# Moving half of GpSimd's adds into an accumulating DMA, and one field from VectorE to ScalarE, in a DLRM tower with a CIN

## The reference

```python
e = stack([tbl_f[ids[:, f]] for f in range(39)], axis=1)     # 512 x 39 x 16
prev = x = e
for k in range(3):                                           # 128 units each
    z = einsum('bmd,bhd->bdmh', x, prev).reshape(b, D, m * h)
    t = transpose(einsum('bdc,co->bdo', z, ws[k]) + bs[k], (0, 2, 1))
    t = t / sqrt(sum(t * t, axis=(-2, -1), keepdims=True))
    logit.append(t); prev = t
z = sum(concatenate(logit, axis=1), axis=-1)
h = relu(concatenate([z, dense_ctx], axis=1) @ W_top1 + b_top1)
y = relu(h @ W_top2 + b_top2) @ W_top3
```

## Time and profile before

| | |
|---|---|
| median of 3 runs | 1061.88 us (1060.4 to 1062.07) |
| profiled execution | 1062.48 us, its span 1060.8 us |
| PE busy | 1028.2 us (97%) |
| PEld busy | 782.4 us (74%) |
| DVE busy | 983.6 us (93%) |
| ACT busy | 791.3 us (75%) |
| POOL busy | 865.9 us (82%) |
| DMA | 46.10 MB, 43 GB/s on average |

### The profile page before, as it was taken

How to read it: one execution, slowest core, us unless ns; L and a number is a source line. 1 busy time by engine, 2 the same in 40 slices (tenths; PEclk the granted TensorE clock), 3 DMA queues, 4 the chain that set the end, 5 groups by cost and what they waited for, 6 DMA issues and landing times.

```text
span 1060.8 us, 17970 instructions
## 1 busy us (share of the span) xinstructions
PE 1028.2 (97%) x4320; PEld 782.4 (74%) x4320; DVE 983.6 (93%) x3344; ACT 791.3 (75%) x2655; POOL 865.9 (82%) x729
## 2 busy tenths in 40 slices
PE   2999999999999999999999999999999999999998
PEld 0477777878777787877778787777878777788884
DVE  2589999999999999999999999999999999999993
ACT  3476877868788786868778687777868778788872
POOL 6777988889898888988888898888889888577770
PEclk9999999999999999999999999999999999999999
DMA  5650030302303030120303012030301203000000
GB/s 188 129 143 12 3 88 3 89 2 52 96 4 88 3 87 4 21 71 2 89 3 87 5 28 64 3 89 2 85 7 17 74 3 89 1 1 1 2 1 1
DMA packets 75892, 46.10 MB, mean 43 GB/s; under 512 B 55689, under 2 KB 58633, under 8 KB 75658
## 3 DMA queue, kind: packets, MB, share of 16 engines
q1 hardware_dynamic: 68487, 38.59, 15.2%
q10 hardware_dynamic: 2179, 5.07, 1.4%
q0 software_dynamic: 5120, 1.29, 1.4%
HBM read 42.99 MB, written 1.94 MB: 42 GB/s over the span
## 4 chain that ended last, share of the span: by engine, by line
PE 48%; POOL 19%; DVE 18%; issue 9%; ACT 5%; DMA 1%; POOLq 0%; DVEq 0%; SPq 0%; ACTq 0%
POOL sums L432 14%; DVE sums L946 12%; PE acc L778 8%; PE bank_d L722 7%; PE bank_d L723 6%; PE bank_d L724 6%; PE bank_a L724 6%; PE bank_a L722 6%; PE bank_a L723 6%; POOL gathered L415 5%; ACT scaled L560 4%; DVE bank_d L946 2%; DVE sums L965 1%; ACT sums L560 1%; PE turned L799 1%
## 5 line engine op out<-in xcount | busy, mean ns | idle before, releaser
L432 POOL TENSOR_TENSOR sums<-sums,scaled 128x512 f32<-128x512 f32 (+1 forms) x512 | 645.1, 1262 | 133.4 <-ACT scaled L560 97.4
L946 DVE SCALAR_TENSOR_TENSOR sums<-bank_d,x_col,sums 128x128 f32<-128x128 f32 x2304 | 654.2, 339 | 29.3 <-PE bank_d L724 20.2
L560 ACT ACTIVATE scaled<-bank_a,x_col 128x128 f32<-128x128 f32 x1920 | 551.5, 385 | 139.8 <-PE bank_a L724 132.7
L722 PE MATMUL bank_d<-w_hi,prev_lo 128*128 128x512 f32 x640 | 288.0, 450 | 6.2 <-DVE sums L965 4.7
L722 PE MATMUL bank_a<-w_hi,prev_lo 128*128 128x512 f32 (+1 forms) x640 | 263.9, 412 | 2.6 <-issue 1.3
L724 PE MATMUL bank_d<-w_hi,prev_hi 128*128 128x512 f32 x640 | 252.5, 394 | 0.0
L723 PE MATMUL bank_d<-w_lo,prev_hi 128*128 128x512 f32 x640 | 252.1, 394 | 0.0
L724 PE MATMUL bank_a<-w_hi,prev_hi 128*128 128x512 f32 (+1 forms) x640 | 245.3, 383 | 0.0
L723 PE MATMUL bank_a<-w_lo,prev_hi 128*128 128x512 f32 (+1 forms) x640 | 245.1, 383 | 0.0
L560 ACT ACTIVATE sums<-bank_a,x_col 128x128 f32<-128x128 f32 x512 | 146.1, 369 | 76.8 <-PE bank_a L724 75.9
L415 POOL DMA_INDIRECT gathered<-in_table,idx x160 | 177.2, 1108 | 28.5 <-issue 18.3
(11 more groups left out here) (84 smaller groups left out, 528.2 us busy)
## 6 DMA issues: line engine op xcount, KB each, us to landing
x_pairs<-x_scratch SPq DMA_DIRECT2D x135, 156.0 KB
x_pairs<-x_scratch SPq DMA_DIRECT2D x96, 78.0 KB
gathered<-in_table,idx POOLq DMA_INDIRECT x160
x_sq<-x_scratch SPq DMA_DIRECT2D x32, 64.0 KB
x_pairs<-x_scratch SPq DMA_DIRECT2D x92, 22.0 KB
x_scratch<-gathered SPq DMA_DIRECT2D x16, 72.0 KB
w_raw<-in_w ACTq DMA_DIRECT2D x1, 1024.0 KB, 5.1
w_raw<-in_w ACTq DMA_DIRECT2D x1, 896.0 KB
```

What stands on the lines that cost most here:

```text
L432: nc.gpsimd.tensor_tensor(out=sums[:, n % SUMS, 0:w, :], in0=sums[:, n % SUMS, 0:w, :], in1=scaled[:, a - 1, 0:w, :], op=ALU.add).then_inc ...
L560: op = nc.scalar.activation(to[:, i, :], bank_a[at % A_RING][:, i * UNITS:(i + 1) * UNITS], ACT.Copy, scale=x_of(c, q, a * PER_BANK + i))
L722: nc.tensor.matmul(to, lo, w_h, start=True, stop=False)
L946: nc.vector.scalar_tensor_tensor(out=taken(n, u) if u in LEFT else total, in0=taken(n, u), scalar=x_of(c, q, A_FIELDS + u), in1=total, op0 ...
```

## The change

In jobs 11 to 116 ("far" jobs) GpSimd no longer adds four slots. It issues one DMA on its own queue that adds slots 3 and 4 onto slots 1 and 2 in SBUF (`accum_op=ALU.add`, 128 partitions of 4096 bytes, 512 KB), and four and five banks later it adds slots 1 and 2 onto `sums`. So that there is time for it, the A banks run ahead by 12 banks instead of 7; the lead grows by one bank a job in jobs 6 to 10 and shrinks again after job 116. Odd far jobs have slots of their own (`scaled_odd`), in the room of the raw weights. GpSimd's gathers move from A places 1 and 2 to 3 and 4 of a job from job 11 on. In all jobs the fields are split 20 to ScalarE and 19 to VectorE, so the bank of three fields is now VectorE's last. The places of `high`, `low`, `make_pairs` and the norms stay.

```diff
-A_FIELDS = A_BANKS * PER_BANK - 1
+A_FIELDS = A_BANKS * PER_BANK
-LEAD = 7
+LEAD, FAR_LEAD = 7, 12
+FAR_FROM, FAR_TO = 11, NJ - 12
+LEADS = [min(max(LEAD, LEAD + n - 5), FAR_LEAD, max(LEAD, FAR_LEAD + FAR_TO - n)) for n in range(NJ + 1)]
+FAR_ADDS = {1: A_BANKS - 1, 2: A_BANKS}
+def a_first(n):
+    return A_BANKS * n + LEADS[n]
+def a_count(n):
+    return a_first(n + 1) - a_first(n) if n + 1 < NJ else A_BANKS
+for _n in range(NJ):
+    for _a in range(1, A_BANKS):
+        if not is_far(_n):
+            ADDS_BEHIND[A_BANKS * _n + _a].append((_n, _a))
+        elif _a in FAR_ADDS:
+            ADDS_BEHIND[A_BANKS * _n + A_BANKS - 1 + FAR_ADDS[_a]].append((_n, _a))
...
+            def add_banks(at):
+                if at >= A_BANKS * NJ:
+                    return
                 n, a = divmod(at, A_BANKS)
-                pool.wait_ge(a_scaled, at + 1)
-                if a > 1:
-                    pool.wait_ge(a_added, ADDS * n + a - 1)
-                w = a_fields_of(a)
-                nc.gpsimd.tensor_tensor(out=sums[:, n % SUMS, 0:w, :], in0=sums[:, n % SUMS, 0:w, :],
-                                        in1=scaled[:, a - 1, 0:w, :], op=ALU.add).then_inc(a_added, 1)
+                if is_far(n) and a == A_BANKS - 1:
+                    pool.wait_ge(a_scaled, at + 1)
+                    nc.gpsimd.dma_start(pair_of(n, 1), pair_of(n, 3), accum_op=ALU.add).then_inc(pair_added[n % 2], 16)
+                for n, a in ADDS_BEHIND[at]:
+                    if is_far(n):
+                        pool.wait_ge(pair_added[n % 2], pairs_added_by(n))
+                    else:
+                        pool.wait_ge(a_scaled, at + 1)
+                    if a > 1:
+                        pool.wait_ge(a_added, ADDED[n, a - 1])
+                    w = PER_BANK if is_far(n) else a_fields_of(a)
+                    nc.gpsimd.tensor_tensor(out=sums[:, n % SUMS, 0:w, :], in0=sums[:, n % SUMS, 0:w, :],
+                                            in1=scaled_of(n, a)[:, 0:w, :], op=ALU.add).then_inc(a_added, 1)
...
-                for a in range(A_BANKS):
-                    add_bank(A_BANKS * n + LEAD + a)
-                    if 1 <= a <= per_step and first + a - 1 < GATHERS:
-                        gather(it + 2, first + a - 1)
+                begin = 1 if n < FAR_FROM else 3
+                for a in range(max(a_count(n), A_BANKS)):
+                    if a < a_count(n):
+                        add_banks(a_first(n) + a)
+                    if begin <= a < begin + per_step and first + a - begin < GATHERS:
+                        gather(it + 2, first + a - begin)
...
-                    if n >= 1:
-                        act.wait_ge(a_added, ADDS * (n - 1) + a)
-                    to = scaled[:, a - 1, :, :]
+                    was = n - 1 if n < FAR_FROM else n - 2
+                    if n == FAR_FROM:
+                        act.wait_ge(w_lo_made[1], len(W_PIECES[1]))
+                        act.wait_ge(w_lo_made[2], len(W_PIECES[2]))
+                    elif is_far(was) and a > max(FAR_ADDS):
+                        act.wait_ge(pair_added[was % 2], pairs_added_by(was))
+                    elif was >= 0:
+                        act.wait_ge(a_added, ADDED[was, a] if (was, a) in ADDED else added_all(was))
+                    to = scaled_of(n, a)
...
-                        bank_for_act(A_BANKS * n + LEAD + a)
-                        a += 1
+                        until = a + 1 if place < len(PATTERN) - 1 else a_count(n)
+                        while a < until:
+                            bank_for_act(a_first(n) + a)
+                            a += 1
...
-                    dve.wait_ge(a_added, ADDS * (n + 1))
+                    dve.wait_ge(a_added, added_all(n))
```

More of the change, by code:

```diff
@@ L46 @@
 D_BANKS = BANKS - A_BANKS
-A_FIELDS = A_BANKS * PER_BANK - 1
+A_FIELDS = A_BANKS * PER_BANK
 D_FIELDS = FIELDS - A_FIELDS
-ADDS = A_BANKS - 1
 LEFT = (D_FIELDS - 3, D_FIELDS - 2)
@@ L200, in cin_kernel @@
         identity = sb("identity", [128, 128])
-        w_raw = {k: sb(f"w{k}_raw", [128, FIELDS, UNITS]) for k in (1, 2)}
+        used = 28
+        with ExitStack() as first_life:
+            w_raw = {k: first_life.enter_context(nc.sbuf_tensor(f"w{k}_raw", [128, FIELDS, UNITS], f32)) for k in (1, 2)}
+        scaled_odd = []
+        for k in (1, 2):
+            sb(f"raw_rows{k}", [128, used, UNITS])
+            scaled_odd.append(sb(f"scaled_odd{k}", [128, 2, PER_BANK, UNITS]))
+            sb(f"raw_rest{k}", [128, FIELDS - used - 2 * PER_BANK, UNITS])
         w_hi = {k: sb(f"w{k}_hi", [128, FIELDS, UNITS], f32r) for k in (1, 2)}
@@ L285, in cin_kernel @@
         a_added = sem("a_added")
+        pair_added = [sem(f"pair_added{parity}") for parity in range(2)]
         d_ready = sem("d_ready")
@@ L323, in cin_kernel, with scaled_of, pair_of, pairs_added_by @@
         TOP_LOADS = 2 * 3 + 2
+        def scaled_of(n, a):
+            if n < FAR_FROM or n % 2 == 0:
+                return scaled[:, a - 1, :, :]
+            return scaled_odd[(a - 1) // 2][:, (a - 1) % 2, :, :]
+        def pair_of(n, a):
+            first = scaled[:, a - 1:a + 1, :, :] if n % 2 == 0 else scaled_odd[(a - 1) // 2][:, :, :, :]
+            return first.rearrange("p a i u -> p (a i u)")[:, 0:(PER_BANK + a_fields_of(A_BANKS - 1)) * UNITS]
+        def pairs_added_by(n):
+            return 16 * ((n - FAR_FROM) // 2 + 1)
         def a_fields_of(a):
@@ L464, in _ @@
                 gather(2, j)
-            for at in range(LEAD):
-                add_bank(at)
+            for at in range(LEADS[0]):
+                add_banks(at)
             for n in range(NJ):
@@ L668, in _ @@
                                  ACT.Copy).then_inc(prev_hi_made[1], 1)
-            for at in range(LEAD):
+            for at in range(LEADS[0]):
                 scale_bank(at)
-                if at == LEAD - 2:
+                if at == LEADS[0] - 2:
                     square_x(1)
             for n in range(NJ):
-                for a in range(A_BANKS):
-                    scale_bank(A_BANKS * n + LEAD + a)
+                for a in range(max(a_count(n), A_BANKS)):
+                    if a < a_count(n):
+                        scale_bank(a_first(n) + a)
                     if (n, a) in W2_HIGH_AT:
```

14 lines of the change are left out of this document (10 added, 4 removed).

## The result

The changed kernel takes 1078.41 us in the median of 4 runs (1075.81 to 1079.59); the kernel before, run beside it, 1061.97 (1060.4 to 1062.07). The ratio is 1.0155 [1.0134, 1.0176]: 1.5% slower. Forecast were 1052.4 us, in a range that ends at 1070. In the profiled executions 16.05 us were added (1062.48 to 1078.53). In the changed kernel the lines have moved: L722 to L724 are now L804 to L806, L946 is L1031, L965 L1050, L914 L999, L432 L503, L437 L508, L560 L641 and L765 L847; L494 is the issue of the accumulating DMA.

A forecast was written before the change was run, and what follows sets the result against it. TensorE was taken as within 2% of its own work, stopped by VectorE. From 1062.48 us, -14.3 (VectorE), -2 and -1 (ends), +7.8 (longer lead) gave 1053.0, as a median 1052.4; 8-in-10 range 1042 to 1070.

The forecast's parts named there:

- The accumulating DMA: GpSimd's new transfer: taken at 4.5 us, some 7 us in the load burst, cost 0, bounds 0 and 39 us.
- VectorE's part: VectorE loses one field a job and `make_pairs` gets shorter; its stops of TensorE vanish, -1.1 us a round, -14.3 us.
- What the longer lead costs: Position 5, first A bank of layer 1: TensorE waits 0.6 us for `prev_lo` in each of 13 rounds, +7.8 us.
- ScalarE's part: ScalarE gains a field a job, 2.1 us a round, 78% busy to 82%; costed at nothing, hidden under idle time.
- GpSimd's part: GpSimd's adds fall from 5.04 to 2.61 us a job plus one DMA issue; load no bound, its order can be.
- Ends: Stretch ahead of job 11, -2 us (0 to -4), and the last job's D banks, -1 us.
- The bound of 5.5 us: GpSimd's loop of issue, transfer and add must fit in 7.78 us; a transfer over 5.5 us makes GpSimd the bound.
- The mild burst form: Rival: only transfers in the load burst are late enough to reach TensorE, some 1.5 us a round, 1072 us; chance 0.08.
- The slow transfer throughout: Rival: a transfer of 6.2 us makes GpSimd's loop the bound in 106 jobs, 1127 us; chance 0.15.
- the floor: Rival: `prev_lo` is in time because ScalarE's queue runs earlier, 1044.6 us; chance 0.17.
- the eaten gain: Rival: `low` is late by another 0.7 us and the new wait eats the gain, 1061.5 us; chance 0.10.
- the last rival: VectorE isn't what stops TensorE, so the change only adds its own wait: within 2 us of 1062; chance within another rival's 0.10.

The follow-up runs named there:

- e3: Changed kernel without the accumulating DMA: slots 3 and 4 of far jobs left out of the sum, lead 12, the split and two adds kept; 1053.95 us, ratio 0.9926.
- e5: Changed kernel with the load burst made small (64-byte rows instead of 2048 from the third chunk on) and the head's weights loaded in round 14; 1056.93 us, ratio 0.9962.
- e7: Changed kernel with the head's weights loaded in round 14 instead of round 3; 1074.37 us, ratio 1.0136.
- e6: Changed kernel with far jobs at positions 0 and 1 added by GpSimd alone, four adds, all other far jobs by the DMA; 1060.81 us, ratio 0.9993.
- e1: Kernel before with only the field split changed, 20 to ScalarE and 19 to VectorE; 1069.0 us, ratio 1.0067.
- e2: Changed kernel with its lead of 12 banks, but GpSimd adds all four slots itself and there is no accumulating DMA; 1107.6 us, ratio 1.0436.
- e4: Changed kernel with `high` and `low` of layer 1 moved from position 5, place 0, to position 4, place 3; 1087.02 us, ratio 1.0237.
- e10: Changed kernel with a lead of 11 banks instead of 12 and the two adds three and four banks behind instead of four and five; 1111.7 us, ratio 1.049.
- e9: Changed kernel with far jobs at positions 0 and 1 added by GpSimd alone and the head's weights loaded in round 14; 1058.24 us, ratio 0.9973.

## Why the prediction was wrong

**The step that failed** is in "The accumulating DMA": "a transfer doubled there to some 7 us is late by 1.5 us in those, and the slack of three D banks takes it up. I cost it at 0". The length was well guessed (median 5.97 us for the burst's first job, 6.57 in the chain of a round, up to 8.2), the upper bound of 39 us held. The cost of 0 didn't. e3 and e5 take the collision away in two ways, one without the transfer and one without the burst, and both give rounds of 61.5 us; with both in place it is 62.6. The collision costs 1.1 us in a steady round, 2.1 to 7.2 in the first three and 0.25 in round 13, some 23 us in sum; the transfers cost another 1.2 us in round 9, with the burst or without it (e5). Of the two jobs a round that the prediction counted only the one at position 0 costs anything: position 1's transfer takes 5.33 us in the median and 8.07 in round 3, and no step after it is longer than in e3. Why the slack didn't hold: it was reckoned from the late transfer alone. In the chain above three more pieces stand behind it on the way to VectorE's bank, the first add of 2.03 us, the issue and the second add of 1.59, where the prediction had taken 1.3 for an add and no lateness handed on: the second add ends 10.8 us after the issue, not 9.2. VectorE waits for 1.45 us, and the slack takes up only half of it, as TensorE's start is late by 0.75. VectorE comes to the bank straight from `make_pairs` and its merges, at 540.80; that its own work had used up the rest of the slack is my reading, which no run singles out.

**What the sum lacked altogether** is the other direction: what the transfers do to the burst. It lasted 10.6 to 12.1 us in the kernel before and 12.6 to 16.7 in the changed one, and 21.5 for 17.0 in round 3, where `make_pairs` waits 4.54 us for its load. No step of the prediction asked when the loads would land. In the later rounds `make_pairs` waits only twice for a load, for 1.4 us together, so this direction costs in round 3 alone: 7.0 us in e7's profile, half clock included (4.0 in the medians), and in e6 3.4 us of the wait are left with the transfers of two positions gone.

**VectorE's part** (-1.1 us a round) was right in size, but laid too much on the field. Without the transfer the stops vanish: e3 gains 0.87 at position 7 to 0, 0.15 at position 1 and 0.09 at position 6, 1.11 together. `make_pairs` has a median of 1.218 us, from 2.190:

```profile
L999 DVE TENSOR_TENSOR z<-x_pairs x46: 1205/1218/2767, 34.3 to 931.8; 128x1024 f32<-128x1024 f32 x30, 117x1024 f32<-117x1024 f32 x16
```

But "get 3 x 0.26 = 0.8 from the field alone" is refuted by e1, where the field alone yields 0.26 us there and costs 1.0 elsewhere. The rest comes with GpSimd's two adds gone: the step from position 7 to 0 takes 7.50 us in e2, with four adds, and 6.91 in e3, with two.

**What the longer lead costs** (+0.6 us a round): right in place and cause, measured as 0.35. e4 and e10 both take it away by making `prev_lo` early enough. TensorE's stop is 0.30 us and the slower start after it:

```profile
521.66 1.30 POOL L508 TENSOR_TENSOR prev_lo<-prev,prev_hi 128x512 fp32r<-128x512 f32 x1 [0.23 <-ACT prev_hi L691]
...
522.49 0.40 PE L806 MATMUL bank_d<-w_hi,prev_hi 128*128 128x512 f32 x1
523.02 0.51 PE L804 MATMUL bank_a<-w_hi,prev_lo 128*128 128x512 f32 x1
```

**ScalarE's part** (0) and **GpSimd's part** held: ScalarE's banks hold TensorE's weight loads up for 4.2 us in 600 (2.1 before), none for over 0.4, and one matmul for 0.7, so the prediction's sign of being wrong, more waits than now, showed without a cost. The issue takes GpSimd 0.93 us on average, against 1.0 taken. It was GpSimd's order and not its load that decided, as that part said.

**Ends** (-2 and -1) failed by some 4 us: in e3 round 1 costs 0.6 us beyond its moved work, round 14 loses 0.65, round 15 gives 0.2 less back than was moved, and the tail gains 0.6: +1 in place of -3.

**The transfer's size** was taken at 4.5 us and is 4.2 to 4.35 alone. The bound of 5.5 us was about right for this order of adds: position 0's transfers of 5.8 to 6.7 us cost 0.9 to 1.25 us a round, the one of 5.14 costs 0.25, and e5's, none over 4.9 there, cost nothing. The prediction let the first add come four banks, 5.5 us, after the issue; in the kernel it comes as soon as the transfer is there. So the sign that went with it, that a first add starting on the DMA means a loss of its wait times 106, was no sign of a loss: e5's adds wait 58.1 us and more in 600 at no cost.

**The rivals.** The mild burst form (0.08) is what happened, in its mechanism; it expected 1.5 us a round and 1072, and 1.1 a round with the first three rounds' excess made 1078. The slow transfer throughout, the floor and the eaten gain didn't come. Against the last rival, that VectorE isn't what stops TensorE, stands e3, where the stops go together with VectorE's load.

**Left open.** Round 9 is longer by 1.2 us at positions 4 and 5 in the changed kernel, in e5 and less in e6, and GpSimd there waits 2 us for one DMA (job 73, in e5 as well) whose packets had ended. And of round 1, whose positions 1 to 5 take 0.8 to 1.4 us more each in e3 too, only the five banks' 3.5 us are explained.

## What to carry to other kernels

A transfer that replaces an engine's work has to be tried against the busiest stretch of the DMA engines, and in both directions: how late it lands itself, and how late it makes the loads that were there. Where it is waited for by an engine that has more to do behind it, its lateness is passed on, so reckon the chain from its landing to the bound engine's next need, with all the pieces between, before slack is set against it. Here it paid, by 0.3%, to use the DMA only in the jobs whose transfers miss the burst and to move other loads out of its way (e9); the first of the two alone was no faster than the kernel before (e6). No run moves those loads in the kernel before, whose round 3 is as short as the others. And relief for one engine was worth nothing until the engine beside it was relieved as well (e1, e3).

## What the runs showed of the hardware

**An accumulating DMA within SBUF moved less than half the bytes a nanosecond of a plain load.** 512 KB land 4.2 to 4.35 us after the start of the issue, the first packet some 1.5 us after it. A packet of 4096 bytes takes a DMA engine 341 ns in the median, a packet of 8192 bytes of the plain loads of weights in the same trace 309 ns: 12 against 26.5 bytes a nanosecond. Those loads come from HBM, and no run has a plain transfer within SBUF beside it, so how much of this is the accumulate isn't shown. The Trainium skill (DMA: Bandwidth & Descriptors, Anatomy of one DMA) led to an estimate of 3.2 us; the measurement says 4.3, and it decides. The same page's section Issuing engines are not separate DMA queues, which spoke against the change, agrees with the trace: 5.97 us in the burst.

**TensorE's clock fell at some of the stops of over 2 us.** In the changed kernel the granted clock was 0.50 for 6.8 us from 286.8 on, within a gap of 5.28 us between two starts, and for 3.4 us from 160.5 on, after one of 2.38; e2 has twelve gaps of 3.3 to 3.5 us and such a stretch at seven of them (mean clock of the run 0.989), here after the one from 528 to 531.5:

```profile
533.05 0.63 PE L793 MATMUL bank_a<-w_hi,prev_lo 128*128 128x512 f32 x1
533.47 0.63 PE L794 MATMUL bank_a<-w_lo,prev_hi 128*128 128x512 f32 x1
533.90 0.63 PE L795 MATMUL bank_a<-w_hi,prev_hi 128*128 128x512 f32 x1
```

It stayed at 1.00 after the stops of up to 1 us of a steady round, and also after e7's gap of 2.25 us at 158 and e10's of 3.21 us at 551.6, shown above; what parts the two kinds isn't shown. Where the clock falls, a stop costs more than its length: in round 3 the stop is 5.05 us, and the 4.5 us at half clock behind it are 2.3 us of work, together about the 7.2 us that the round takes over e3. Such a stretch appears in some executions at the start as well (6.8 us in e3's profile). Of the 13 executions of the kernel before that ran beside e9, the six with a mean clock of 0.998 took 1061.6 to 1063.5 us, the seven with 1.000 took 1059.7 to 1061.6, so this is part of the scatter of about 2 us.
